# Layer-1 attention scores: from two 128-row products on the whole array to three 64-row products in two row tiles, issued two tiles at a time

## Time and profile before

| | |
|---|---|
| median of 3 runs | 717.78 us |
| profiled execution | 718.75 us |
| its span in the trace | 717.0 us |
| busy PE / DVE / ACT / POOL | 702.8 / 537.0 / 454.7 / 229.2 us |
| layer 1: 512 score matmuls, first and last start | 268.7 and 695.5 us |

### The profile page before, as it was taken

The page is one execution under the profiler, slowest core; times in us unless marked ns, Lnnn a source line. Parts: engine busy times, 40 slices in busy tenths (PEclk is TensorE's granted clock), DMA queues, the critical chain, the costliest instruction groups (busy, mean ns, idle before and its releaser), DMA issues.

```text
span 717.0 us, 11953 instructions
## 1 busy us (share of the span) xinstructions
PE 702.8 (98%) x3924; PEld 597.0 (83%) x3924; DVE 537.0 (75%) x878; ACT 454.7 (63%) x820; POOL 229.2 (32%) x214
## 2 busy tenths in 40 slices
PE   7999999999999999999999999999999999999996
PEld 6888888888888887878888888888887888888886
DVE  3565465456547728999888899888889888889994
ACT  4552254145226507789777789777778878778882
POOL 0120021012013303365333456333356423334440
PEclk9999999999999999999999999999999999999999
DMA  8000210040030175500257210256401165301010
GB/s 277 2 2 30 89 57 15 29 132 0 34 126 16 51 171 137 143 0 1 75 139 181 78 55 6 68 139 148 117 17 41 44 143 126 100 15 45 16 45 30
DMA packets 29101, 52.74 MB, mean 74 GB/s; under 512 B 3456, under 2 KB 5760, under 8 KB 29056
## 3 DMA queue, kind: packets, MB, share of 16 engines
q1 hardware_dynamic: 29056, 52.19, 26.3%
HBM read 18.62 MB, written 8.39 MB: 38 GB/s over the span
## 4 chain that ended last, share of the span: by engine, by line
PE 88%; DVE 4%; ACT 3%; issue 2%; DMA 1%; SPq 0%; ACTq 0%; DVEq 0%
PE acc L1096 45%; PE scores L1096 26%; PE trans L1130 18%; DVE negmax L778 2%; DMA w_later<-in_wlater 1%; DVE pt_lo L796 1%; ACT prob L585 1%; ACT pt_hi L595 1%; DVE o_sum L999 0%; ACT o_sum L699 0%; ACT h_hi L643 0%; DVE gn_sqdev L832 0%; DVE rsum L783 0%; SPq L385 0%; SPq L380 0%
## 5 line engine op out<-in xcount | busy, mean ns | idle before, releaser
L505 POOL TENSOR_SCALAR prob<-prob,rsum 128x1024 f32<-128x1024 f32 x159 | 179.2, 1127 | 469.1 <-DVE rsum L783 469.1
L595 ACT ACTIVATE pt_hi<-trans 128x512 fp32r<-128x512 f32 x320 | 174.8, 595 | 129.2 <-PE trans L1130 126.7
L778 DVE TENSOR_REDUCE negmax<-scores 128x1 f32<-128x1024 f32 x160 | 194.2, 1214 | 45.6 <-PE scores L1096 44.0
L796 DVE TENSOR_TENSOR pt_lo<-trans,pt_hi 128x512 fp32r<-128x512 f32 x320 | 204.5, 680 | 9.3 <-ACT pt_hi L595 9.0
L585 ACT ACTIVATE prob<-scores,negmax 128x1024 f32<-128x1024 f32 x160 | 179.1, 1120 | 30.1 <-DVE negmax L778 28.5
L1130 PEld LDWEIGHTS trans<-ident,prob 128*128 128x128 f32 x1280 | 147.0, 140 | 32.2 <-DVE pt_lo L796 5.1
L1130 PE MATMUL trans<-ident,prob 128*128 128x128 f32 x1280 | 168.7, 274 | 3.8 <-DVE pt_lo L796 3.2
L1096 PE MATMUL scores<-k_st,q_st 128*128 128x512 f32 x512 | 137.8, 391 | 0.0
L1096 PEld LDWEIGHTS scores<-k_st,q_st 128*128 128x128 f32 x512 | 95.9, 188 | 20.8 <-ACT prob L585 0.2
L1096 PE MATMUL acc<-pt_hi,v_st 128*128 128x512 f32 (+1 forms) x264 | 108.0, 410 | 1.8 <-DVE pt_lo L796 1.8
L1096 PE MATMUL acc<-pt_lo,v_st 128*128 128x512 f32 (+1 forms) x264 | 102.4, 389 | 0.0
(11 more groups left out here) (121 smaller groups left out, 893.9 us busy)
## 6 DMA issues: line engine op xcount, KB each, us to landing
k_st<-qk SPq DMA_DIRECT2D x64, 256.0 KB, 4.8
q_st<-qk SPq DMA_DIRECT2D x64, 128.0 KB, 2.4
x_raw<-in_x SPq DMA_DIRECT2D x8, 512.0 KB, 6.9
y_out<-in_x SPq DMA_DIRECT2D x16, 256.0 KB, 3.9
y_scratch<-y_out SPq DMA_DIRECT2D x16, 256.0 KB, 2.0
y_in<-y_scratch SPq DMA_DIRECT2D x4, 1024.0 KB, 7.5
y_res<-y_scratch SPq DMA_DIRECT2D x16, 256.0 KB, 3.8
out<-y_res SPq DMA_DIRECT2D x16, 256.0 KB, 2.0
```

The source lines that it names most:

```text
L505: nc.gpsimd.tensor_scalar(p, p, rsum[:, t % 2:t % 2 + 1], 1.0, ALU.mult, ALU.mult)\
L595: nc.scalar.activation(pt_block(pt_hi, (t // 4) % 2, t, h), trans[:, h, :].rearrange("p (j n) -> p j n", n=P), ACT.Copy).then_inc(pt_high, 1)
L778: nc.vector.tensor_reduce(negmax[:, t % 2:t % 2 + 1], scores[:, t % 2, :], AX_X, ALU.max, negate=True).then_inc(max_ready, 1)
L796: nc.vector.tensor_tensor(pt_block(pt_lo, slot, t, h), trans[:, h, :].rearrange("p (j n) -> p j n", n=P), pt_block(pt_hi, slot, t, h).bitc ...
```

## The change

Each 64-row part stands in its own half of the partitions. `q_st` becomes `[P, 2, HEADS, N]`: both parts of q, each copied to partitions 0-63 and to 64-127. `k_st` becomes `[P, 2, HEADS, H]`: the first half of the keys in partitions 0-63, the second half in 64-127. `scores1` runs the three terms high*high, low*high, high*low (`products`), and for each term one matmul on rows 0-63 (keys 0 to 511) and one on rows 64-127 (keys 512 to 1023): six matmuls of 64 rows and 512 columns for each tile.

On even steps PE issues the scores of tiles s+2 and s+3 one after the other, on odd steps none. On odd steps ACT does `exp(s+2)` before `trans_high(s)`; on even steps after it, as before. DVE's and POOL's orders are not touched. A q chunk is moved by four DMAs of 256 KB, a k chunk by two of 256 KB; the semaphore counts follow.

```diff
-        q_st = sb("q_st", [P, HEADS, N], F32R)
-        k_st = sb("k_st", [P, 2, HEADS, N], F32R)
+        q_st = sb("q_st", [P, 2, HEADS, N], F32R)
+        k_st = sb("k_st", [P, 2, HEADS, H], F32R)
...
-        CHUNK_DMA = 4 * 16
-        QK_IMAGE = 4 * CHUNK_DMA
+        Q_DMA, K_DMA = 4 * 16, 2 * 16
+        QK_PAIR = Q_DMA + K_DMA
+        QK_IMAGE = PAIRS * QK_PAIR
+
+        def stacked_before(r):
+
+            return (r // 4) * QK_PAIR + (Q_DMA if r % 4 >= 2 else 0)
...
                 for n in range(2):
-                    head, rows = 2 * pair + n, slice(n * HD, (n + 1) * HD)
-                    for u in range(2):
-                        if is_k:
-                            dst, src = k_st[u * HD:(u + 1) * HD, :, head, cols], qk[rows, slot, :, :]
-                        else:
-                            dst, src = q_st[u * HD:(u + 1) * HD, head, cols], qk[rows, slot, u, :]
+                    head, src = 2 * pair + n, qk[n * HD:(n + 1) * HD, slot, :, :]
+                    if is_k:
+                        homes = [k_st[half * HD:(half + 1) * HD, :, head, :]]
+                    else:
+                        homes = [q_st[u * HD:(u + 1) * HD, :, head, cols] for u in range(2)]
+                    for dst in homes:
                         sp.dma_start(dst.bitcast(F32), src.bitcast(F32)).then_inc(qk_stacked[slot], 16)
...
-                act.wait_ge(qk_stacked[r % 2], FREE_CREDIT + QK_IMAGE * i + CHUNK_DMA * (r // 2))
+                act.wait_ge(qk_stacked[r % 2], FREE_CREDIT + QK_IMAGE * i + stacked_before(r))
...
+                    exp_ahead = s + LAG < T1_IMAGE or not plan.last
+                    if exp_ahead and s % 2 == 1:
+                        exp(t1, s + LAG)
                     trans_high(t1, s, before)
-                    if s + LAG < T1_IMAGE or not plan.last:
+                    if exp_ahead and s % 2 == 0:
                         exp(t1, s + LAG)
...
-                for mh in range(2):
-                    ins = run(scores[:, s % 2, col(mh, H)],
-                              [(q_st[:, head, col(tile, P)], k_st[:, part, head, col(mh, H)]) for part in range(2)])
+
+                terms = products((q_st[:, 0], k_st[:, 0]), (q_st[:, 1], k_st[:, 1]))
+                for n, (q, k) in enumerate(terms):
+                    for mh in range(2):
+                        rows = slice(mh * HD, (mh + 1) * HD)
+                        ins = nc.tensor.matmul(scores[:, s % 2, col(mh, H)], q[rows, head, col(tile, P)], k[rows, head, :],
+                                               start=n == 0, stop=n == len(terms) - 1)
                 ins.then_inc(scores_ready, 1)
...
-                    if s + LAG < T1_IMAGE:
-                        scores1(i, t1, s + LAG)
-                    elif not plan.last:
-                        scores1(i + 1, t1 + T1_IMAGE, s + LAG - T1_IMAGE)
+                    if s % 2 == 0:
+                        for ahead in (s + LAG, s + LAG + 1):
+                            if ahead < T1_IMAGE:
+                                scores1(i, t1, ahead)
+                            elif not plan.last:
+                                scores1(i + 1, t1 + T1_IMAGE, ahead - T1_IMAGE)
```

More of the change, by code:

```diff
@@ L1198, in scores1 @@
                     for slot in range(2):
-                        pe.wait_ge(qk_stacked[slot], FREE_CREDIT + QK_IMAGE * i + CHUNK_DMA * (2 if s == 0 else 4))
+                        pe.wait_ge(qk_stacked[slot], FREE_CREDIT + QK_IMAGE * i + QK_PAIR * (1 if s == 0 else 2))
                 pe.wait_ge(exp_ready, t1 + s + 1)
-                for mh in range(2):
-                    ins = run(scores[:, s % 2, col(mh, H)],
-                              [(q_st[:, head, col(tile, P)], k_st[:, part, head, col(mh, H)]) for part in range(2)])
+                terms = products((q_st[:, 0], k_st[:, 0]), (q_st[:, 1], k_st[:, 1]))
[4 more added lines that the diff above has]
+                                               start=n == 0, stop=n == len(terms) - 1)
                 ins.then_inc(scores_ready, 1)
```

## The result

| | us |
|---|---|
| before, median of 4 runs | 717.41 |
| after, median of 4 runs (795.05 to 797.8) | 797.25 |
| ratio | 1.1116, 95% interval 1.1092 to 1.1139 |
| span of the profiled execution, before and after | 717.0 and 793.3 |

The kernel became slower by 11.2%.

What follows compares the result with a forecast made beforehand. PE bounds the kernel before; after, a DVE-ACT ring of 6.96 us a pair does. Terms 71.0 + 4 + 2.8 + 1.8 = 79.6 on 718.75 give 798.4, stated as 797 against the median; range 768 to 812.

Steps and rivals of the forecast that it cites:

- The ring of a pair: Layer 1, two steps: closed loop of DVE and ACT waits between even row maxima, 6.96 us against PE's 5.46 before.
- What lies in the ring: DVE's evacuations of qk, v and out before a row_max add 46.2 us; `o_sum` additions on even steps add 11.5.
- The stretch: Row_max of tile 2 to that of tile 127: 491.8 us against 420.8 before, +71.0.
- the turns: Between images: ACT's fetch and a q chunk's DMA now get in the way, +4 us of 0 to 9.
- What lies behind the last maximum: Kernel's end: trans_low of tile 125 and the last two transposes come later, +1.8 us (0 to 2).
- the term of the DMAs: Layer 0's tail: ACT's copies wait for larger q DMAs, +2.8 us, bounds 0 and 4.
- Row tiles run side by side: Score matmuls on PE: two 64-row tiles in parallel, 0.69 us for each tile, saving PE 29.4 us.
- a change between 128 and 64 rows: On PE: each change of tiling mode costs 0.08 us, 10 us in all, cutting PE's saving from 29 to 19.
- rival A: PE stays last everywhere and only its sum counts, so the kernel gets faster: 698 us; chance 0.05.
- B: The 6.96 us pair holds, but evacuations and additions slip into its waits: 740, half of them 768; chance 0.12.
- C: Score matmuls' row tiles run one behind the other on PE: 800 to 804 us; chance 0.10.
- D: PE's idle pieces in pairs without further groups drop the clock to its lower level: above 850 us; chance 0.02.

Runs made afterwards that it cites:

- the run on one row tile: 64-row products alone, ACT's old order, with all six matmuls of a tile on rows 0 to 63 and keys 0 to 511: 817.94 us, ratio 1.1437.
- the paired kernel: Kernel before with one edit, two tiles' scores at once on even steps; 128-row products, old DMAs, ACT's old order: 755.99 us, ratio 1.0553.
- the unpaired 64-row kernel: Kernel before with only the 64-row products and new DMAs; one tile's scores on every step, ACT's old order: 736.79 us, ratio 1.0281.

## Why the prediction was right

**The ring of a pair.** Given 6.96, measured 6.96 (474.37 to 481.33), link by link within 0.01. DVE's wait before the odd `pt_lo` was given as about 1.8 and is 1.84. That the order of ACT alone makes it was argued then; the run with nothing but the swap shows it. One comparison in the forecast is off without changing it: before, a light pair takes 5.28 between even maxima and not PE's 5.46, since DVE and ACT set their pace.

**What lies in the ring.** A pair with an `o_sum` was given 6.96 + 0.37 = 7.33; from 467.07 to 474.37 it is 7.30. For a pair with two groups I gave 8.8, and 8.3 where the even one is an output; counted between even maxima, the five of the second image take 8.78, 8.76, 8.41 (the one with the output), 8.79 and, at its end, 9.41, which has an `o_sum` as well.

**The stretch.** From the maximum of tile 2 to that of tile 127 I gave 491.8, and 4 for the turns; it is 772.58 - 278.14 = 494.4. The two rows:

```profile
278.14 1.21 DVE L786 TENSOR_REDUCE negmax<-scores 128x1 f32<-128x1024 f32 x1
...
772.58 1.20 DVE L786 TENSOR_REDUCE negmax<-scores 128x1 f32<-128x1024 f32 x1
```

Against the earlier trace rows that is +73.7 (given 71.0 and 4, so 75.0). What lies behind the last maximum grew by 0.4 (given 1.8). What lies ahead of tile 2 grew by 278.14 - 275.89 = 2.3 (given 2.8), but that number hides two others. The first row maximum of layer 0 in the two executions:

```profile
22.36 1.22 DVE L778 TENSOR_REDUCE negmax<-scores 128x1 f32<-128x1024 f32 x1
...
20.58 1.23 DVE L786 TENSOR_REDUCE negmax<-scores 128x1 f32<-128x1024 f32 x1
```

In the execution before it comes 1.8 later, ahead of anything that the change touches: from 15 to 20 us its granted clock was 0.66, and 1.00 in the one after. From that maximum to tile 2's it is 253.5 before and 257.6 after. So the term of the DMAs is 4.0, its upper bound, and not 2.8.

The three together are 76.3, the difference of the spans. The medians differ by 79.8, since the profiled execution before, 718.75, was above all four of its runs and the one after, 795.05, was the shortest of its four. The sum of the forecast was 79.6, which is 3.3 too high between spans: 1.3 too much for the stretch, 1.4 for the end and 1.8 for the late start, less 1.2 too little for the DMAs. That the forecast met the median to 0.3 us is luck of that kind; that it came within a few us is not.

**The turns and the DMAs.** The mechanism was half right. In layer 0's tail ACT's copies of chunks 2 and 3 wait for q's DMAs, as worked out:

```profile
251.28 0.69 ACT L642 ACTIVATE qk<-acc,vec 128x512 fp32r<-128x512 f32 x1 [3.51 <-DMA q_st<-qk]
256.98 0.69 ACT L642 ACTIVATE qk<-acc,vec 128x512 fp32r<-128x512 f32 x1 [5.01 <-DMA q_st<-qk]
```

The working let q's DMAs of 256 KB land 2.4 us after their issue, as the old ones of 128 KB do. They take longer:

```profile
q_st<-qk SPq DMA_DIRECT2D x64, 256.0 KB, 4.6
```

Of the 4.0, 3.8 are there when ACT copies the next chunk (268.49, and 264.60 in the 128-row kernel with the same orders, whose layer 0 starts 0.1 earlier), before the first 64-row matmul at 271.0. The 4.0 stands in every kernel with the 64-row products of both key halves and PE's scores ahead of the transposes (257.4 to 257.6 from layer 0's first maximum to tile 2's), and in none with 128 rows (253.5 in all five).

Between the images the time is not spread over three turns. Only the turn from the second image to the third is the end of a pass through the loop in the program; the others are straight code. The pair there takes 10.66 after and 7.69 in the 128-row kernel with the same orders, so 3.0 go with the new products and DMAs.

**PE.** Here the working was off, where it didn't count. Row tiles run side by side, as I took it, but a change between 128 and 64 rows costs PE 0.18 and not 0.08, which had been read at the av matmuls behind the transposes, where the number of rows doesn't change. By that a paired kernel gains 0.48 - 0.37 = 0.11 a pair on PE, 7 us in all, and rival A's 698 was not to be had even with a free DVE. The Trainium skill, "TensorEngine Tiling (Array Packing)", Key Properties, says that changing the mode drains the engine: the traces agree, with 0.36 to 0.37 before the first weight load of either kind.

**The rivals.** A (PE stays last) fell with the change without the 64-row products, where more work on PE costs nothing. B (evacuations slip into the waits) fell by the pairs of 7.30 and 8.8. C (row tiles one behind the other) fell by the run on one row tile. D: the clock stayed at 0.99 to 1.00 in all four windows of 120 us of layer 1, so PE's idle pieces in the light pairs did not lower it. These means hide one place: at the turn PE was idle 4.05 us until 537.01, and the granted clock of the next window was 0.57.

```profile
531.00:536.00 5.00, 1.96 (x12) 1.44 (x12) 2.51 (x5) 0.97 (x2) 1.12 (x1) 1.00 1.06 222
536.00:540.00 4.00, 2.99 (x12) 2.75 (x13) 2.57 (x4) 2.56 (x5) 1.12 (x1) 0.57 0.53 138
```

## What to carry to other kernels

Before two instructions of an engine change places, write down the ring through all engines that each of them is in, start to start, and count what stands queued behind the one that will wait. Busy shares don't show it: the kernel had an engine at 98%, and an order on another engine at 63% cost 76 us. And when work is moved ahead of its time, its waits are moved too. Before an order is changed to relieve a wait, see whether the instruction waits for that at all: in the paired kernel's light pairs the odd exponential already started 1.32 after its maximum, so the swap relieved nothing there and added a ring.

## What the runs showed of the hardware

A 64-row matmul of 512 columns takes PE as long as one of 128 rows, 0.23 from start to start; two on different halves of the rows share that time, even when three for one half are queued before three for the other. At a change between the two shapes the next weight load does not start while the matmul before it runs: 0.36 to 0.37 of idle time before the weight load, and 0.18 on PE's step.

At the loop's turn ACT was idle with nothing recorded that it waited for, 2.03 in the kernel before; the prediction takes this for the fetch of its next instructions, which no run tells apart. In the changed kernel it is 4.03. In the unpaired 64-row kernel the same turn falls together with q's larger DMAs, and the idle time is 3.93; PE then waits for `pt_lo`:

```profile
505.36 1.09 ACT L600 ACTIVATE pt_hi<-trans 128x512 fp32r<-128x512 f32 x2 [3.93 <-issue]
...
506.73 1.52 PE L1135 MATMUL trans<-ident,prob 128*128 128x128 f32 x8 [2.93 <-DVE pt_lo L801]
```

Windows of that kernel around it: length, busy times, granted clock, DMA share, GB/s.

```profile
502.00:507.00 5.00, 2.07 (x12) 1.14 (x12) 2.35 (x5) 1.64 (x3) 1.13 (x1) 1.00 1.05 217
507.00:514.00 7.00, 7.00 (x36) 5.36 (x35) 4.93 (x9) 4.12 (x9) 2.25 (x2) 0.76 0.19 57
```

The DMA engines were full while ACT waited (share 1.05; 1.06 in the changed kernel), and after PE had been idle 2.93 the granted clock fell: 0.76 as a mean of the next 7 us, between the levels of 1.2 and 2.4 GHz. That ACT's longer wait comes from the DMAs is what the coincidence suggests; I ran nothing that shows it.
